# Cross-attention of a Perceiver layer: probabilities turned ahead of the scores in every step, and copied ahead of the maximum

## The chip, the cores and the metric

The kernel runs on one core of one Trainium2 chip. Its engines work side by side, each through its own instructions in order: TensorE (PE, and PEld for its weight loads), VectorE (DVE), ScalarE (ACT), GpSimd (POOL) and SyncE (SP), which issues the loads and stores. They wait for each other by semaphores. The metric is the device time of one execution in microseconds (us), and the number that is compared is the median of several executions.

## What is computed

The layer has three parts: cross-attention of 4096 rows over a context, causal self-attention, and a mixture of 8 experts. The change touches the first part alone.

```python
def _L0_xattn_ref(x, context, Wq, Wk, Wv, Wo, bo):
    HEADS = 16; DIM_HEAD = 64; SCALE = DIM_HEAD ** (-0.5)
    q = x @ Wq            # x: 64 x 64 x 256
    k = context @ Wk      # context: 64 x 256 x 192
    v = context @ Wv
    ...                   # each split into 16 heads of 64
    sim = jnp.einsum('bhid,bhjd->bhij', q, k) * SCALE
    attn = jax.nn.softmax(sim, axis=-1)
    out = jnp.einsum('bhij,bhjd->bhid', attn, v)
    out = out.transpose(0, 2, 1, 3).reshape(B, Nq, INNER_DIM)
    return out @ Wo + bo

x = x + _L0_xattn_ref(_layernorm(x), ctx_768, ...)   # then self-attention, then the experts
```

## The kernel before

Rows are worked on in tiles of 128, that is two batches of 64 rows with 256 keys each, so there are 32 tiles, and two tiles (u = 0 and u = 1) make a group. `run_tiles` writes group 0 out (its first tile is special, `first=True`), runs a loop of 14 times over groups 1 to 14, writes group 15 out, and ends with a short drain. A tile is 8 steps p = 0 to 7, one for each pair of heads, and there are 16 steps in a group.

Products that need more than one pass are made of a rounded part (hi) and a rest (lo). Keys are never projected: the key weights are absorbed into the queries. For each pair and each half h there is one such unit of work, here called an absorption: TensorE multiplies `q_sb` by `wkt` into the bank `qk_ps` (or `o_ps`, for the three that are called early), ScalarE rounds it into `qk_hi` (`absorbed_hi`), and VectorE writes the rest into `qk_lo` and `qk_hi` (`absorbed_lo`, two instructions). Only then may TensorE put the next absorption into `qk_ps`: `absorb` waits for `qk_done`.

What TensorE does in a step of a tile that is not the first, in this order (`tile` under `@block.tensor`):

- the scores of the pair before, ten matmuls into one of two banks `s_ps` (`scores`)
- in some steps the projection of a query pair, six matmuls into `m_ps` (`project_q`; steps 0, 2, 4 of u = 0 and 0, 1, 2, 4, 6 of u = 1)
- the values, five matmuls into `v_ps`
- in steps 1 and 2 of u = 1 an early absorption into `o_ps`
- the transposes of the probabilities of the pair three back, four into `t_ps` (line 555). They wait for `norm_done` from GpSimd two steps back and for `t_done`, VectorE's copy of the transposes before
- in steps 3 and 7 the product of probabilities and values, 64 matmuls into `o_ps` (line 571)
- in step 4 the output projection, 24 matmuls into `y_ps`
- in nearly all steps of u = 0 but the last, and of u = 1 but the first, a late absorption into `qk_ps`, the last work of the step

VectorE in a step: the negated maximum of the scores (`nmax`, line 733), the rest of the absorption that TensorE made at the end of the step before (`unit_behind`), the rest of the projected query (`q_lo`), the rest of an early absorption, in one step of a group `xt_lo`, the copy of the transposes from `t_ps` to `pt_sb` (line 754), the reciprocal of the sums (line 757, after ScalarE's exponentials), and what belongs to single steps: `ot_lo` in steps 3 and 7, the output rows in 5, `rem_lo` in 6, the layer norm of the next group in steps 0 (statistics) and 2 of u = 0.

ScalarE in a step: the rounded part of the absorption behind, of the projected query (`q_hi`), the two exponentials (line 667), the copy of the values, the rounded part of an early absorption. GpSimd scales the probabilities by the reciprocal (line 412). The order is written by hand; in all engines it is program order.

Of the kernel before, what the change touches and what calls it, by code (L numbers as in the profile page):

```python
# [22 lines left out]
P = 128  # L23
# [7 lines left out]
def wait(eng, sem, value):  # L31

    if isinstance(value, int) and value <= 0:
        return
    eng.wait_ge(sem, value)
# [38 lines left out]
def layer_kernel(nc, x, ctx_t, wq, wk, wv, wo, bo, sq, sk, sv, so, router, w_gate, w_up, w_down, out):  # L74
# [7 lines left out]
    PAIRS = E // P  # L82
# [8 lines left out]
    with ExitStack() as root:  # L91
# [9 lines left out]
        ident = sbuf(root, "ident", [P, P])  # L101
# [113 lines left out]
        with ExitStack() as ph:  # L215
# [229 lines left out]
            def _(pe):  # L445
# [66 lines left out]
                def tile(t, u, first, last, look, drain=False):  # L512
                    for p in range(PAIRS):
# [7 lines left out]
                        if first and p == 1:  # L521
                            pe.wait_ge(s_ctx, 3)
                            pe.wait_ge(s_rem, 1)
                        if (not first if p < LAG_S else cur):
                            scores(t, u, p, n, w)
# [22 lines left out]
                        if p == PAIRS - 1 and u == 0 and look:  # L548
                            turn_x(t // 2 + 1)
                        if (not first if p < LAG_T else cur):  # L550

                            pe.wait_ge(norm_done, n - 2)
                            wait(pe, t_done, n - 3)
                            for k in range(4):
                                mm = pe.transpose(t_ps[:, k * P:(k + 1) * P],  # L555
                                                  p_sb[:, (p - 3) % 4, k * P:(k + 1) * P], ident[:])
                            mm.then_inc(t_mm, 1)
                        if p % 4 == 3 and (not first if p < LAG_PV else cur):
# [138 lines left out]
            def _(dve):  # L697
# [24 lines left out]
                def tile(t, u, first, last, look, drain=False):  # L722
                    for p in range(PAIRS):
# [5 lines left out]
                        if first:  # L729
                            absorbed_lo(*early[:3], two_banks=True)  # L730
                        if (not first if p < LAG_S else cur):
                            dve.wait_ge(s_mm, n)
# [14 lines left out]
                        if p == PAIRS - 1 and u == 0 and look:  # L747
                            xt_lo_copy(t // 2 + 1)
                        if (not first if p < LAG_T else cur):
                            dve.wait_ge(t_mm, n - 2)  # L750
                            wait(dve, pv_mm, PAIRS * t - (0 if p >= LAG_PV else 4))
                            if first and p == LAG_T:
                                weights.wait_split(dve, O_SPLIT)
                            nc.vector.tensor_copy(pt_sb[:, PT_SLOT[(p - 3) % PAIRS], :], t_ps[:]).then_inc(t_done, 1)  # L754
                        if (not first if p < LAG_S else cur):
# [1016 lines left out]
```

## Time and profile before

| | us |
|---|---|
| median of 3 runs | 2334.02 |
| lowest and highest | 2332.64, 2343.82 |
| the profiled execution | 2338.02 |
| its span, first to last instruction | 2336.3 |
| PE busy in the span | 2202.6 |
| DVE busy | 1595.0 |
| ACT busy | 1283.4 |

The profiled execution is 4.0 us above the median. Cross-attention goes from the start to about 1236 us, self-attention to about 1880, the experts to the end. Within cross-attention one group of 16 steps follows the other: from the scores of step 4 at 501.06 us to the same place at 575.55 us it is 74.5 us. Matmuls are pipelined, so their durations overlap; the pace of TensorE is read from start to start.

### The profile page before, as it was taken

The numbers are of one execution on the slowest core, as the hardware profiler recorded it, in microseconds if no ns is written. First come the engines' busy times: TensorE is split into PE (matmuls) and PEld (weight loads), VectorE is DVE, ScalarE is ACT, GpSimd is POOL, SyncE is SP. The second block draws the span as 40 slices with busy tenths as digits, with TensorE's granted clock in tenths as the row PEclk, the third lists the DMA queues.
The fourth block names the chain that finished last, engine by engine and source line by source line (L and its number), as shares of the span: only waits on it lengthen the run. The fifth ranks groups of instructions, "written<-read, shape, count | busy, mean of one in ns | idle before, by whom it ended". The sixth has DMA issues, their size and how long they took to land. (4 is left out here: it accounts for less than half of the span.)

```text
span 2336.3 us, 55684 instructions
## 1 busy us (share of the span) xinstructions
PE 2202.6 (94%) x18992; PEld 1991.8 (85%) x18992; DVE 1595.0 (68%) x3591; ACT 1283.4 (55%) x3842; POOL 847.2 (36%) x1022
## 2 busy tenths in 40 slices
PE   6999999999999999999996999999999956999995
PEld 5899999999999999999985999999999844888884
DVE  6666676766667676666655888888898756444442
ACT  5555555555555555555544666676766622444442
POOL 3333333333333333333331222222222223777673
PEclk9999999999999999999997999999999976999998
DMA  4000000000000000000004000000000011434434
GB/s 115 19 20 27 9 27 27 18 27 9 27 18 27 13 22 27 18 27 9 14 6 154 11 10 18 9 18 9 18 9 19 19 39 48 105 79 104 78 54 104
DMA packets 61946, 82.52 MB, mean 35 GB/s; under 512 B 9936, under 2 KB 45520, under 8 KB 61808
## 3 DMA queue, kind: packets, MB, share of 16 engines
q1 hardware_dynamic: 48912, 63.46, 8.6%
q0 software_dynamic: 12960, 18.12, 4.7%
q8 instruction: 40, 0.66, 0.1%
q14 instruction: 34, 0.28, 0.0%
HBM read 59.80 MB, written 25.96 MB: 37 GB/s over the span
## 5 line engine op out<-in xcount | busy, mean ns | idle before, releaser
L412 POOL TENSOR_TENSOR p_sb<-p_sb,rinv 128x512 f32<-128x512 f32 x256 | 279.5, 1092 | 781.3 <-DVE rinv L757 781.3
L667 ACT ACTIVATE p_sb<-s_ps,nmax 128x256 f32<-128x256 f32 x512 | 238.3, 470 | 198.7 <-DVE nmax L733 194.8
L733 DVE TENSOR_REDUCE nmax<-s_ps 128x2 f32<-128x512 f32 x256 | 176.3, 689 | 186.6 <-PE s_ps L65 182.2
L914 POOL TENSOR_TENSOR sp_sb<-sp_sb,srinv 128x512 f32<-128x512 f32 x128 | 133.4, 1042 | 426.1 <-DVE srinv L1108 426.1
L1056 ACT ACTIVATE sp_sb<-sm_sb,snmax 128x128 f32<-128x128 f32 x512 | 199.4, 390 | 7.1 <-DVE snmax L1119 4.0
L754 DVE COPY pt_sb<-t_ps 128x512 f32<-128x512 f32 x256 | 177.0, 691 | 22.1 <-PE t_ps L555 8.5
L46 ACT ACTIVATE q_sb<-m_ps 64x256 fp32r<-64x256 f32 x256 | 97.0, 379 | 164.1 <-PE m_ps L65 160.3
L45 ACT CAST qk_hi<-qk_ps 128x512 fp32r<-128x512 f32 x218 | 129.8, 595 | 96.1 <-PE qk_ps L65 88.3
L555 PE MATMUL t_ps<-ident,p_sb 128*128 128x128 f32 x1024 | 153.8, 273 | 2.1 <-POOL p_sb L412 1.1
L555 PEld LDWEIGHTS t_ps<-ident,p_sb 128*128 128x128 f32 x1024 | 125.0, 141 | 31.8 <-issue 4.5
L638 ACT COPY v_sb<-v_ps 128x512 f32<-128x512 f32 x256 | 149.4, 584 | 1.5 <-PE v_ps L65 1.5
L65 PE MATMUL s_ps<-cx_hi,qk_hi 128*128 128x256 f32 x512 | 148.4, 290 | 0.0
L65 PE MATMUL qk_ps<-q_sb,wkt_hi 128*128 128x256 f32 x436 | 131.8, 324 | 14.3 <-DVE qk_hi L57 6.0
L65 PE MATMUL s_ps<-cx_lo,qk_hi 128*128 128x256 f32 x512 | 145.0, 283 | 0.0
L65 PE MATMUL s_ps<-cr_lo,qk_hi 128*128 128x256 f32 x512 | 144.9, 283 | 0.0
L65 PE MATMUL s_ps<-cx_hi,qk_lo 128*128 128x256 f32 x512 | 144.8, 283 | 0.0
L65 PE MATMUL s_ps<-cr_hi,qk_hi 128*128 128x256 f32 x512 | 144.8, 283 | 0.0
L571 PEld LDWEIGHTS o_ps<-pt_sb,v_sb 128*64 128x64 f32 x4096 | 126.2, 139 | 11.6 <-issue 10.5
L571 PE MATMUL o_ps<-pt_sb,v_sb 128*64 128x64 f32 x4096 | 135.1, 225 | 0.8 <-DVE pt_sb L754 0.8
L58 DVE SCALAR_TENSOR_TENSOR q_sb<-m_ps,q_sb 64x256 fp32r<-64x256 f32 x256 | 108.1, 422 | 37.6 <-ACT q_sb L46 30.9
L1570 POOL DMA_INDIRECT acc<-e_ys,e_token_out x67 | 107.3, 1601 | 23.1 <-issue 18.6
L65 PE MATMUL qk_ps<-q_sb,wkt_lo 128*128 128x256 f32 x436 | 113.9, 283 | 0.0
(300 smaller groups left out, 7581.7 us busy)
## 6 DMA issues: line engine op xcount, KB each, us to landing
ctx_raw<-in_ctx_t SPq DMA_DIRECT2D x32, 256.0 KB, 2.8
ctx_raw<-in_ctx_t SPq DMA_DIRECT2D x64, 128.0 KB, 3.0
x_ring<-in_x SPq DMA_DIRECT2D x16, 256.0 KB, 2.8
x_mid<-x_ring SPq DMA_DIRECT2D x16, 256.0 KB, 2.2
xn<-f_xn SPq DMA_DIRECT2D x16, 256.0 KB, 2.2
acc<-x_sb SPq DMA_DIRECT2D x16, 256.0 KB, 2.3
e_raw<-in_gate SPq DMA_DIRECT2D x8, 512.0 KB
e_raw<-in_up SPq DMA_DIRECT2D x8, 512.0 KB
```

Of the source, the lines that this page charges most:

```text
L45: return nc.scalar.copy(hi, src)
L58: return nc.vector.scalar_tensor_tensor(out=lo, in0=src, scalar=scale, in1=f32(hi), op0=ALU.mult, op1=ALU.subtract)
L65: mm = pe.matmul(out, lhs, rhs, start=(i == 0), stop=(i == len(pairs) - 1))
L412: nc.gpsimd.tensor_tensor(prob, prob, inv, ALU.mult).then_inc(norm_done, 1)
L555: mm = pe.transpose(t_ps[:, k * P:(k + 1) * P], p_sb[:, (p - 3) % 4, k * P:(k + 1) * P], ident[:])
L571: mm = pe.matmul(o_ps[h * HEAD:(h + 1) * HEAD, c:c + HEAD], v_sb[:, k, q * P + h * HEAD:q * P + (h + 1) * HEAD], pt_sb[:, PT_SLOT[q], k * ...
L638: nc.scalar.copy(v_sb[:, p % 4, p // 4 * HALF:(p // 4 + 1) * HALF], v_ps[:]).then_inc(v_done, 1)
L667: ex = nc.scalar.activation(p_sb[:, k, b * J:(b + 1) * J], s_ps[1 - w][:, b * J:(b + 1) * J], ACT.Exp, bias=nmax[:, k, b:b + 1], scale=1.0 ...
L733: nc.vector.tensor_reduce(nmax[:, (p - 1) % 4, :], s_ps[1 - w][:].rearrange("p (b j) -> p b j", b=2), AX_X, ALU.max, negate=True).then_inc ...
L754: nc.vector.tensor_copy(pt_sb[:, PT_SLOT[(p - 3) % PAIRS], :], t_ps[:]).then_inc(t_done, 1)
L914: nc.gpsimd.tensor_tensor(prob, prob, inv, ALU.mult).then_inc(norm_done, 1)
L1056: ex = nc.scalar.activation(p_sb[:, s, k * P:(k + 1) * P], sm_sb[:, w, k * P:(k + 1) * P], ACT.Exp, bias=nmax[:, s, k:k + 1], scale=1.0, a ...
```

## The change

On TensorE the block of four transposes moves from behind the values (and the early absorption) to the head of the step, ahead of `scores`. On VectorE the copy of these transposes moves from behind the rests to ahead of the maximum. No instruction is added or taken away, and all semaphores and the values that are waited for stay.

```diff
@@ TensorE, tile @@
+                        if (not first if p < LAG_T else cur):
+
+                            pe.wait_ge(norm_done, n - 2)
+                            wait(pe, t_done, n - 3)
+                            for k in range(4):
+                                mm = pe.transpose(t_ps[:, k * P:(k + 1) * P],
+                                                  p_sb[:, (p - 3) % 4, k * P:(k + 1) * P], ident[:])
+                            mm.then_inc(t_mm, 1)
                         if (not first if p < LAG_S else cur):
                             scores(t, u, p, n, w)
...
-                        if (not first if p < LAG_T else cur):
-
-                            pe.wait_ge(norm_done, n - 2)
...
@@ VectorE, tile @@
+                        if (not first if p < LAG_T else cur):
+                            dve.wait_ge(t_mm, n - 2)
+                            wait(dve, pv_mm, PAIRS * t - (0 if p >= LAG_PV else 4))
+                            if first and p == LAG_T:
+                                weights.wait_split(dve, O_SPLIT)
+                            nc.vector.tensor_copy(pt_sb[:, PT_SLOT[(p - 3) % PAIRS], :], t_ps[:]).then_inc(t_done, 1)
                         if (not first if p < LAG_S else cur):
                             dve.wait_ge(s_mm, n)
...
-                            nc.vector.tensor_copy(pt_sb[:, PT_SLOT[(p - 3) % PAIRS], :], t_ps[:]).then_inc(t_done, 1)
```

TensorE, end of step 5 and start of step 6 of a tile u = 1, before (`qk_ps` is the late absorption, `s_ps` the first of the next step's scores, the names in brackets are the semaphores waited for):

```order
L65 MATMUL v_ps<-wv_rem,cr_lo 128x512
L555 MATMUL t_ps<-ident,p_sb 128x128 [waits x_t_copied,x_norm]
L555 MATMUL t_ps<-ident,p_sb 128x128 x3
L65 MATMUL qk_ps<-q_sb,wkt_hi 128x256 [waits x_qk_split,x_q_split]
L65 MATMUL qk_ps<-q_sb,wkt_lo 128x256
L65 MATMUL qk_ps<-q_sb,wkt_hi 128x256
L65 MATMUL qk_ps<-q_sb,wkt_lo 128x256
L65 MATMUL s_ps<-cx_hi,qk_hi 128x256 [waits x_exp]
```

The same place after the change:

```order
L65 MATMUL v_ps<-wv_rem,cr_lo 128x512
L65 MATMUL qk_ps<-q_sb,wkt_hi 128x256 [waits x_qk_split,x_q_split]
L65 MATMUL qk_ps<-q_sb,wkt_lo 128x256
L65 MATMUL qk_ps<-q_sb,wkt_hi 128x256
L65 MATMUL qk_ps<-q_sb,wkt_lo 128x256
L529 MATMUL t_ps<-ident,p_sb 128x128 [waits x_t_copied,x_norm]
L529 MATMUL t_ps<-ident,p_sb 128x128 x3
L65 MATMUL s_ps<-cx_hi,qk_hi 128x256 [waits x_exp]
```

The transposes no longer stand between the values and the late absorption, but between the late absorption and the next scores.

VectorE, steps 5 and 6 of a tile u = 1 before, from the maximum of step 5 on:

```order
L733 TENSOR_REDUCE nmax<-s_ps 128x2 [waits x_s_mm]
L57 TENSOR_TENSOR qk_lo<-qk_ps,qk_hi 128x4x64 [waits x_qk_hi]
L57 TENSOR_TENSOR qk_hi<-qk_ps,qk_hi 64x4x64
L754 COPY pt_sb<-t_ps 128x512 [waits x_pv_mm,x_t_mm]
L757 RECIPROCAL rinv<-rsum 128x2 [waits x_exp]
L764 TENSOR_TENSOR x_ring<-y_ps,x_ring 128x256 [waits x_y_mm]
L733 TENSOR_REDUCE nmax<-s_ps 128x2 [waits x_s_mm]
```

The same place after, from the copy of step 5 on:

```order
L736 COPY pt_sb<-t_ps 128x512 [waits x_pv_mm,x_t_mm]
L739 TENSOR_REDUCE nmax<-s_ps 128x2 [waits x_s_mm]
L57 TENSOR_TENSOR qk_lo<-qk_ps,qk_hi 128x4x64 [waits x_qk_hi]
L57 TENSOR_TENSOR qk_hi<-qk_ps,qk_hi 64x4x64
L757 RECIPROCAL rinv<-rsum 128x2 [waits x_exp]
L764 TENSOR_TENSOR x_ring<-y_ps,x_ring 128x256 [waits x_y_mm]
```

The copy stands ahead of the maximum, and the reciprocal follows the rests directly.

## Rows read from the trace of the kernel before

**Rows 1.** The page's first part: busy time, share of the span, instructions.
```profile
PE 2202.6 (94%) x18992; PEld 1991.8 (85%) x18992; DVE 1595.0 (68%) x3591; ACT 1283.4 (55%) x3842; POOL 847.2 (36%) x1022
```

**Rows 2.** Stretches: length, PE, PEld, DVE, ACT, POOL busy, PEclk, DMA share, GB/s.
```profile
20.00:60.00 40.00, 31.68 (x198) 28.66 (x199) 32.36 (x68) 24.56 (x59) 9.33 (x11) 1.00 0.22 64
...
427.50:1171.50 744.00, 740.12 (x7239) 680.24 (x7238) 507.52 (x1122) 415.57 (x1170) 260.53 (x250) 1.00 0.07 20
```

**Rows 3.** Waits from 60 to 1225 us: total us, times, longest.
```profile
DVE nmax L733 <- PE s_ps L65: 181.7, 143, 3.6
...
PEld qk_ps L65 <- DVE qk_hi L57: 17.5, 56, 0.7
PEld o_ps L571 <- issue: 10.5, 63, 0.2
...
PE qk_ps L65 <- DVE qk_hi L57: 6.0, 14, 0.4
```

**Rows 4.** TensorE in time, steps 5 and 6 of u = 1: start, length, instruction.
```profile
544.66 0.28 PE L65 MATMUL qk_ps<-q_sb,wkt_hi 128*128 128x256 f32 x1
...
545.14 0.28 PE L65 MATMUL s_ps<-cx_hi,qk_hi 128*128 128x256 f32 x1
...
546.34 0.40 PE L65 MATMUL v_ps<-wv_hi,cx_hi 128*128 128x512 f32 x1
...
547.51 0.60 PE L555 MATMUL t_ps<-ident,p_sb 128*128 128x128 f32 x4
548.06 0.39 PE L65 MATMUL qk_ps<-q_sb,wkt_hi 128*128 128x256 f32 x1
...
548.64 0.28 PE L65 MATMUL s_ps<-cx_hi,qk_hi 128*128 128x256 f32 x1
...
552.08 0.36 PE L65 MATMUL qk_ps<-q_sb,wkt_hi 128*128 128x256 f32 x1
```

**Rows 5.** VectorE in time, step 5 of the same tile; in brackets the idle time before.
```profile
546.54 0.69 DVE L733 TENSOR_REDUCE nmax<-s_ps 128x2 f32<-128x512 f32 x1 [3.55 <-PE s_ps L65]
547.15 0.42 DVE L57 TENSOR_TENSOR qk_lo<-qk_ps,qk_hi 128x256 fp32r<-128x256 f32 x1
547.58 0.43 DVE L57 TENSOR_TENSOR qk_hi<-qk_ps,qk_hi 64x256 fp32r<-64x256 f32 x1
548.14 0.69 DVE L754 COPY pt_sb<-t_ps 128x512 f32<-128x512 f32 x1
```

**Rows 6.** TensorE, then VectorE, in group 15, where scores follow transposes directly.
```profile
1192.35 0.60 PE L555 MATMUL t_ps<-ident,p_sb 128*128 128x128 f32 x4
1192.70 0.36 PE L65 MATMUL s_ps<-cx_hi,qk_hi 128*128 128x256 f32 x1
...
1194.18 0.69 DVE L733 TENSOR_REDUCE nmax<-s_ps 128x2 f32<-128x512 f32 x1 [0.43 <-PE s_ps L65]
```

**Rows 7.** Steps 0 and 1 of u = 0, with the layer norm: ScalarE, VectorE, TensorE.
```profile
561.95 0.20 ACT L667 ACTIVATION_READ_ACCUMULATOR p_sb<-s_ps,nmax 128x1 f32 x1
...
562.75 0.17 DVE L757 RECIPROCAL rinv<-rsum 128x2 f32<-128x2 f32 x1
...
563.98 0.69 DVE L733 TENSOR_REDUCE nmax<-s_ps 128x2 f32<-128x512 f32 x1
...
565.50 0.39 PE L65 MATMUL qk_ps<-q_sb,wkt_hi 128*128 128x256 f32 x1 [0.43 <-DVE qk_hi L57]
```

**Rows 8.** VectorE in step 2 of u = 1, then TensorE's late absorption.
```profile
530.60 0.67 DVE L733 TENSOR_REDUCE nmax<-s_ps 128x2 f32<-128x512 f32 x1
...
531.62 0.43 DVE L57 TENSOR_TENSOR qk_hi<-qk_ps,qk_hi 64x256 fp32r<-64x256 f32 x1
...
532.24 0.36 PE L65 MATMUL qk_ps<-q_sb,wkt_hi 128*128 128x256 f32 x1
```

**Rows 9.** GpSimd in time: the scaling of the probabilities whose scores began at 545.14.
```profile
549.11 1.04 POOL L412 TENSOR_TENSOR p_sb<-p_sb,rinv 128x512 f32<-128x512 f32 x1 [5.00 <-DVE rinv L757]
```

**Rows 10.** A stretch in the drain; columns as in rows 2.
```profile
1225.60:1229.40 3.80, 3.68 (x64) 3.50 (x64) 0.01 (x1) 0.00 (x1) 0.00 (x0) 0.50 0.02 4
```

More of the change, by code:

```diff
@@ L549, in tile @@
                             turn_x(t // 2 + 1)
-                        if (not first if p < LAG_T else cur):
-                            pe.wait_ge(norm_done, n - 2)
[L553 to L557, printed above, removed]
                         if p % 4 == 3 and (not first if p < LAG_PV else cur):
@@ L748, in tile @@
                             xt_lo_copy(t // 2 + 1)
[L749 to L753, printed above, removed]
-                            nc.vector.tensor_copy(pt_sb[:, PT_SLOT[(p - 3) % PAIRS], :], t_ps[:]).then_inc(t_done, 1)
                         if (not first if p < LAG_S else cur):
```

## The prediction

> **What bounds the kernel now.** The page comes first: TensorE is busy 94% of the span [rows 1]. The stretches then say where: over ten groups of cross-attention, 744 us, it is busy 740 at full clock, so the stage is paced by TensorE, and only what makes it wait or work longer can move the time [rows 2]. The list of waits names the one thing that it waits for in the steady loop: an absorption's first weight load waits for VectorE's second rest (`qk_hi`), 56 times, 17.5 us in all, that is 4 times in each of 14 groups [rows 3]. In the other direction VectorE waits for the scores before its maximum, 143 times, 181.7 us [rows 3].
>
> The timelines of TensorE and VectorE side by side explain this wait. In step 5 of u = 1 the scores start at 545.14, the maximum at 546.54, the two rests at 547.15 and 547.58, the second ends at 548.01, and the late absorption starts at 548.06 [rows 4, 5]. From the scores' start to the absorption that is a chain of 2.92 us, all of it forced: the maximum waited for the scores (idle 3.55 before), the rests stand behind the maximum, the absorption needs its bank freed. In the meantime TensorE issues scores (1.20), values (1.17) and transposes (547.51 on, 0.35 as from 1192.35 to 1192.70 in [rows 6]), 2.72 in sum. It is 0.20 short, and waits. So the transposes are what TensorE does while VectorE works through the chain; this is what the change takes away.
>
> **The tight steps.** After the change such a step is transposes, scores, values, then the absorption. The scores start 0.35 later, and the chain starts with them. It also grows a little: where scores follow transposes, the maximum starts 1.48 after them and not 1.40 [rows 4 to 6], since the first matmul runs longer (0.36 against 0.28). The step, from its first work to the next step's first, was 3.50 (545.14 to 548.64 [rows 4]); it becomes 0.35 + 2.92 + 0.08 + 0.58 (absorption to next step, 548.06 to 548.64) = 3.93, so +0.43. TensorE then stands idle some 0.6 in it. VectorE's copy doesn't lengthen the chain there: it can start 0.63 after the transposes (547.51 to 548.14 [rows 4, 5]) and lasts 0.69, so it is over at 1.32, and the maximum is due at 0.35 + 1.48 = 1.83; what hides the copy is VectorE's wait for the scores. Such steps have no projection, no product of 64 and no output projection between scores and absorption: steps 5 and 6 of u = 0 and step 5 of u = 1, three in each of 15 groups. 45 x 0.43 = **19.4 us**. Bounds: 0.35 (the longer first matmul is gained back elsewhere) and 0.55, 15.8 to 24.8.
>
> The Trainium skill bears on the 0.08: "TensorE: Matmul & The Clock Gate", Part 2, says that the engine's window pulls a weight load ahead of the matmuls in flight, so that it is hidden. By that rule the 0.08 would be zero and this term 15.8; the rows show it behind transposes.
>
> **The layer-norm step.** In steps 0 and 1 of u = 0 VectorE is late already: between reciprocal (562.75) and maximum (563.98) lie the layer norm's statistics, 1.23, with no idle time, and the absorption waits 0.43 [rows 7]. Now the copy comes between statistics and maximum: +0.72 (a copy and its distance to the next instruction). But the reciprocal no longer stands behind the copy; it needs the exponentials, ready at 562.15 [rows 7] and now 0.35 later, as the projection ahead of them moves back, so it can start near 562.55, 0.2 earlier. The maximum then starts at 562.55 + 1.23 + 0.72 = 564.50, with 0.06 for one more instruction of the sequencer between them 0.58 later than before, and so does the absorption, which waits for it. 14 x 0.58, and group 15 without statistics 0.43: **8.5 us**. Bounds 0.36 and 1.1 each, 5 to 15.
>
> **Steps 1 and 2 of u = 1.** VectorE has its longest backlog here: two queries' and two absorptions' rests. The maximum at 530.60 follows other work directly, and the second rest ends at 532.05, while the absorption that needs it started at 532.24, just unstalled [rows 8]; there is no fifth wait in a group [rows 3]. The chain behind this is projection, ScalarE's part, rests, copy, maximum; its head, the projection, now comes 0.35 after the step's start, where it had come first thing behind the scores. The rest ends near 0.4 later, which makes the absorption 0.2 to 0.35 late; I take 0.3. 15 x 0.3 = **4.5 us**. Bounds 0 (the second copy is out of the way) and a whole copy, 0.7: 0 to 10.
>
> **Steps that only trade places.** With a projection in it the step is not tight: in step 6 TensorE comes to the absorption 3.44 after the scores (548.64 to 552.08 [rows 4]), 3.09 without the transposes, 3.17 with the longer first matmul, and the chain needs 3.00. The cover is thin, 0.17 us: if it goes, three such steps a group (0 and 2 of u = 0, 6 of u = 1) cost what the chain lacks. An absorption behind values instead of transposes reaches the next step in 0.48 (544.66 to 545.14 [rows 4]) and not 0.56, which pays for the 0.08. The output projection of step 4 covers everything: 0. In the steps with the product of 64, TensorE now goes to it from the values. The trace has a gap of 0.17 ahead of each product, 10.5 us in 63 [rows 3], always behind transposes, whose matmuls are short. Whether it stays behind the longer values no row shows: -0.10 if it goes, +0.08 if it stays, times 62, so -6 to +5. I take **-1**.
>
> **First tile and drain.** Two stretches without the loop's rhythm. In the first tile VectorE is busy 32.4 of 40 us [rows 2] and paces it; the copy filled its pause between two absorptions and now lies in its chain, five steps from p = 3 on, some 0.5 each: **2.5 us** (0 to 3.5). In the drain the last scores' maximum waits behind one more copy, and the last transposes wait for the end of its chain, with nothing beside it: a copy's 0.69 [rows 5], **0.7 us**.
>
> **The waits that are only moved.** The transposes' own condition, `norm_done`, must now hold earlier. The scaling of the probabilities of scores 545.14 runs from 549.11 to 550.15 [rows 9]; its transposes are those of step 7, which starts at about 552.6. Over 2 us are left, so nobody waits. Behind them queue the scores, so this would be dear if it failed. No DMA moves: SP waits for `s_ctx`, `s_rem` and `bo_added`, which come from GpSimd work with idle time before it (5.00 us [rows 9]).
>
> **Sum.** 19.4 + 8.5 + 4.5 - 1 + 2.5 + 0.7 = 34.6. The profiled execution took 2338.0, so 2372.6; the median of the runs is 2334.0, 4.0 lower, and that is what will be compared: 2368.6. I say 2368.
>
> **The rivals.**
> - *The wait is VectorE's backlog, not the chain.* If the absorption waited because VectorE was still behind from copies of the step before, a copy moved into its idle time before the maximum would end the wait, and the kernel would gain up to all 17.5 of PEld's wait, 2317. It decides whether the maximum starts late or on time. On time in the tight steps (idle 3.55 before it [rows 5]), late only in the layer-norm step; against it. Chance 0.03.
> - *Nothing to measure.* The stalls come, but are paid back: the gap of 0.17 vanishes (-6), a step that stalls lets VectorE catch up, and the late steps cost nothing. 15.8 + 5 + 0 - 6 - 5 = about 10, 2344. Chance 0.07. That the change doesn't do what it says is out: the order shows the absorption right behind the values.
> - *The thin cover breaks.* If the 45 steps with a projection and no other cover also wait, and lose as much as the tight ones do, 0.4 each, that is 18 us more, 2386. For it: the cover is 0.17, and VectorE has further work in them. Against it: that work stands behind the rests, not ahead. Chance 0.09.
> - *The clock falls.* TensorE now pauses 0.6 us several times a group. In the trace the granted clock stays 1.00 from 20 to 60 us though TensorE is idle a fifth of it [rows 2]; at 0.50, in the drain, the product of 64 takes 3.68 us [rows 10]. A twentieth of the stage at that level would cost some 58 us, 2426. Chance 0.02. The Trainium skill, in the same page under "A second HAM failure mode: psum-queue depth-cycling", says that frequent short pauses between groups of matmuls make the clock swing between its levels; by this trace they don't.
>
> **How the numbers follow.** The forecast, 2350 to 2383, has the remaining 0.79. The low bounds, 15.8 + 5 + 0 - 6 + 0 + 0.7, give 15.5, so 2350; the high ones together would be 59, but not all at once, and I stop at 50, 2384. Range 2350 to 2384. The measurement tells about 0.5% (11.7 us) from no change: slower than that 0.90, within 0.07, faster 0.03.
>
> **What would show it.** In the profile after, a group takes 76.3 to 77 us and not 74.5; PEld's wait for `qk_hi` rises from 17.5 to some 50, in five steps a group and not four, about 0.6 in the tight ones; the maximum still starts 1.48 after the scores in steps 5 and 6; the granted clock of the loop is 1.00; PEld waits for no `p_sb`. If the group is not longer, the chain was not forced; if `o_ps` has no gap any more, that term goes down by 5.

## The result, and the profile after

The changed kernel takes 2377.48 us, the median of 4 runs (2373.95 to 2379.01); the kernel before, run beside it, 2334.56 (2332.64 to 2343.82). The ratio is 1.017, with a 95% interval of 1.015 to 1.0188: slower by 42.9 us. 2368 was forecast, 34.6 above the kernel before. The profiled execution took 2377.52, and its span is 2375.8.

First the page of the changed kernel, its part on busy time, to set against [rows 1]; then the stretches, as in [rows 2] (length, PE, PEld, DVE, ACT, POOL busy, PEclk, DMA share, GB/s), of which the long one is ten groups again:

```profile
PE 2205.7 (93%) x18992; PEld 1985.9 (84%) x18992; DVE 1591.9 (67%) x3591; ACT 1281.2 (54%) x3842; POOL 847.0 (36%) x1022
```

```profile
20.00:60.00 40.00, 31.54 (x211) 28.33 (x211) 32.89 (x70) 23.78 (x57) 9.88 (x11) 1.00 0.20 64
427.50:1197.00 769.50, 743.93 (x7250) 678.97 (x7249) 508.79 (x1125) 416.12 (x1171) 262.95 (x251) 1.00 0.06 19
```

The same numbers of instructions do the same work in the same busy time. What is new is idle time of TensorE: 25.6 us in ten groups, where it was 3.9 in [rows 2]. A group takes 76.95 us instead of 74.5, and the granted clock of TensorE is 1.00 in both stretches as the rows print it; for 20 to 60 us the matmuls say otherwise (see the rivals, below).

The list of waits of the changed kernel from 60 to 1225 us (total, times, longest) names the place, beside [rows 3]:

```profile
DVE pt_sb L736 <- PE t_ps L529: 110.0, 76, 2.9
...
DVE nmax L739 <- PE s_ps L65: 63.1, 137, 0.5
PEld qk_ps L65 <- DVE qk_hi L57: 59.2, 56, 1.8
...
PE qk_ps L65 <- DVE qk_hi L57: 38.9, 74, 1.3
...
PEld o_ps L571 <- issue: 19.3, 61, 0.4
...
DVE ln_stats_x L164 <- issue: 3.0, 14, 0.2
```

The absorption's wait for VectorE's second rest is the one that grew: from 17.5 to 59.2 us on PEld, and from 14 to 74 times on PE, which is some five a group. VectorE's long wait is now at its copy, the first thing in a step that needs TensorE, and no longer at the maximum. No wait for the scaled probabilities is in the list up to 1225 us.

A tight step of the changed kernel, step 5 of u = 1, on TensorE (start, length, instruction, in brackets the idle time), against [rows 4]:

```profile
558.71 0.60 PE L529 MATMUL t_ps<-ident,p_sb 128*128 128x128 f32 x4
559.06 0.36 PE L65 MATMUL s_ps<-cx_hi,qk_hi 128*128 128x256 f32 x1
...
560.33 0.40 PE L65 MATMUL v_ps<-wv_hi,cx_hi 128*128 128x512 f32 x1
...
562.05 0.38 PE L65 MATMUL qk_ps<-q_sb,wkt_hi 128*128 128x256 f32 x1 [0.39 <-DVE qk_hi L57]
...
562.63 0.60 PE L529 MATMUL t_ps<-ident,p_sb 128*128 128x128 f32 x4
```

and VectorE in the same step, against [rows 5]:

```profile
559.34 0.69 DVE L736 COPY pt_sb<-t_ps 128x512 f32<-128x512 f32 x1 [2.92 <-PE t_ps L529]
560.53 0.69 DVE L739 TENSOR_REDUCE nmax<-s_ps 128x2 f32<-128x512 f32 x1 [0.50 <-PE s_ps L65]
561.14 0.41 DVE L57 TENSOR_TENSOR qk_lo<-qk_ps,qk_hi 128x256 fp32r<-128x256 f32 x1
561.57 0.43 DVE L57 TENSOR_TENSOR qk_hi<-qk_ps,qk_hi 64x256 fp32r<-64x256 f32 x1
```

From transposes to transposes it is 3.92 us, with the scores at 0.35, the maximum 1.47 behind them, and the absorption 2.99 behind them. The copy is over at 560.03, and VectorE still waits 0.50 for the scores: the copy costs nothing here. The values' last matmul starts near 561.27 (560.33 and four of 0.23), so TensorE has some 0.55 with nothing new to start.

The layer-norm step of the changed kernel, on VectorE, against [rows 7], and then on TensorE:

```profile
576.59 0.17 DVE L757 RECIPROCAL rinv<-rsum 128x2 f32<-128x2 f32 x1 [0.19 <-ACT p_sb L667]
576.97 0.75 DVE L164 BATCH_NORM_STATS2 ln_stats_x<-x_ring 128x6 f32 x2 [0.21 <-issue]
...
578.24 0.69 DVE L736 COPY pt_sb<-t_ps 128x512 f32<-128x512 f32 x1
578.85 0.68 DVE L739 TENSOR_REDUCE nmax<-s_ps 128x2 f32<-128x512 f32 x1
```

```profile
576.44 0.36 PE L65 MATMUL s_ps<-cx_hi,qk_hi 128*128 128x256 f32 x1
...
580.35 0.39 PE L65 MATMUL qk_ps<-q_sb,wkt_hi 128*128 128x256 f32 x1 [1.31 <-DVE qk_hi L57]
...
581.28 0.36 PE L65 MATMUL s_ps<-cx_hi,qk_hi 128*128 128x256 f32 x1
```

TensorE waits 1.31 for the rest, where [rows 7] had 0.43. From scores to scores this step takes 4.84 us; before, the same places are 562.11 and 566.07, 3.96.

### The profile page after: what moved, and what is told of

The parts are those of the page before. It is cut to its first block and busy times, and to the rows that moved or that the text cites. A ratio compares the mean times of both kernels' runs of the same rounds, so it can differ in the third digit from the quotient of the medians.

```text
span 2375.8 us, 55684 instructions
## 1 busy us (share of the span) xinstructions
PE 2205.7 (93%) x18992; PEld 1985.9 (84%) x18992; DVE 1591.9 (67%) x3591; ACT 1281.2 (54%) x3842; POOL 847.0 (36%) x1022
## 5 line engine op out<-in xcount | busy, mean ns | idle before, releaser
L65 PE MATMUL qk_ps<-q_sb,wkt_hi 128*128 128x256 f32 x436 | 126.0, 311 | 48.4 <-DVE qk_hi L57 38.9
L65 PE MATMUL s_ps<-cx_hi,qk_hi 128*128 128x256 f32 x512 | 164.7, 322 | 0.0
L65 PEld LDWEIGHTS qk_ps<-q_sb,wkt_hi 128*128 128x128 f32 x436 | 82.3, 189 | 88.2 <-DVE qk_hi L57 59.2
L58 DVE SCALAR_TENSOR_TENSOR q_sb<-m_ps,q_sb 64x256 fp32r<-64x256 f32 x256 | 108.1, 422 | 36.8 <-ACT q_sb L46 30.2
L529 PEld LDWEIGHTS t_ps<-ident,p_sb 128*128 128x128 f32 x1024 | 118.3, 140 | 6.8 <-POOL p_sb L412 2.5
```

What stands on the lines that cost most here:

```text
L58: return nc.vector.scalar_tensor_tensor(out=lo, in0=src, scalar=scale, in1=f32(hi), op0=ALU.mult, op1=ALU.subtract)
L65: mm = pe.matmul(out, lhs, rhs, start=(i == 0), stop=(i == len(pairs) - 1))
L529: mm = pe.transpose(t_ps[:, k * P:(k + 1) * P], p_sb[:, (p - 3) % 4, k * P:(k + 1) * P], ident[:])
```

## The experiments

The theory is the chain of the prediction: scores, maximum, two rests, absorption. It sets the length of some steps, and more so since the transposes no longer stand inside it. A length of a step is given below from the start of its values to the start of the next step's values, unless it says otherwise; on that measure a tight step is 3.49 before and 3.92 after (4.22 and 4.65 where it holds the next step's projection).

The first five kernels move both parts in some steps of a tile only. Their edit is one condition, and both blocks stand in both places, under it and under its opposite:

```diff
+            def ahead(t, u, p, first, drain):
+                return not first and not drain and (u, p) in ((0, 5), (0, 6), (1, 5))
...
+                        if ahead(t, u, p, first, drain) and (not first if p < LAG_T else cur):
+                            pe.wait_ge(norm_done, n - 2)
...
-                        if (not first if p < LAG_T else cur):
+                        if not ahead(t, u, p, first, drain) and (not first if p < LAG_T else cur):
```

**The three tight steps alone.** The edit is the one shown.

> The new order (transposes ahead of the scores, copy ahead of the maximum) in three steps of a group only: 5 and 6 of u = 0 and 5 of u = 1, that is 45 steps; all else as before. My theory (the transposes were what TensorE did while VectorE worked through maximum and rests, 2.92 us, and moved ahead they lengthen the step by themselves and the slower first matmul): each such step 3.93 instead of 3.50, a group 75.8 instead of 74.5, the kernel +19.4 us, near 2354. Rival (the copy on VectorE, and not the transposes' place, costs the time, and costs it in the steps where VectorE is late): these steps have VectorE idle before the maximum, so they stay at 3.50 and the kernel at 2334.6.

Measured: 2359.54 us (2357.66 to 2361.2, 4 runs) beside 2337.87; ratio 1.0089 (1.0061 to 1.0117). A group takes 75.73 us, +1.24, which is 3 x 0.41. From the first scores to the last transposes the stage is 19.1 us longer. The waits of this kernel from 60 to 1225 us:

```profile
DVE nmax L751 <- PE s_ps L65: 96.1, 141, 1.1
...
PEld qk_ps L65 <- DVE qk_hi L57: 44.2, 56, 0.8
```

PEld's wait goes up by 26.7 us, with the maximum waiting for the scores about as often as before (141 times for 143). The forecast of 19.4 for this part holds.

**Steps 0 and 1 of u = 0 alone** (`u == 0 and p < 2`), the layer-norm step.

> The new order in steps 0 and 1 of u = 0 only, where the layer norm's statistics stand between reciprocal and maximum. My theory: the changed kernel's trace shows 4.84 from the scores of step 1 to those of step 2 instead of 3.97, of which the copy between statistics and maximum is 0.6 to 0.7 and the rest the wait of the statistics' own instructions (0.38 from reciprocal to statistics, 0.08 before), which the copy had hidden; so 14 x 0.87 and 0.43 in group 15: +12.6 us, near 2347. Rival (the steps lose only what the transposes' place takes, 0.43 as in any tight step): 15 x 0.43 = +6.4 us, near 2341.

Measured: 2351.56 us (2347.18 to 2354.1, 5 runs), ratio 1.006 (1.0038 to 1.0082). The group is 75.34, +0.85, and the stage 12.5 longer. `DVE ln_stats_x <- issue: 3.0, 14, 0.2` is in its list, as in the changed kernel's and not in the list of before.

**Steps 1 and 2 of u = 1 alone** (`u == 1 and p in (1, 2)`).

> The new order in steps 1 and 2 of u = 1 only, where VectorE has two absorptions' and two queries' rests. My theory: the absorption at the end of step 2 waits about 0.5 us for a rest that now ends later; 15 x 0.31 = +4.7 us, near 2339, and the group 74.8 instead of 74.5. Rival (the changed kernel's longer step 2 is a consequence of the steps before it): with the steps before and after in the old order nothing is left, 2334.6.

Measured: 2366.51 us (4 runs), ratio 1.0124 (1.0096 to 1.0151); group 76.08, +1.6 and not +0.31. The expectation was missed, and its waits show why:

```profile
PEld t_ps L533 <- issue: 20.1, 16, 1.3
...
PE t_ps L533 <- DVE pt_sb L772: 16.8, 16, 1.1
```

Where step 0 is in the old order and step 1 in the new one, the transposes of the two stand almost side by side, and there is one bank `t_ps`. The second four wait for the copy of the first, 1.1 us, once a group. This wait belongs to the seam and is in neither whole kernel, so the run says nothing about the term.

**All steps but these** (the opposite of the three conditions together, first tile and drain included).

> The new order in all steps but those three sets (5, 6, 0, 1 of u = 0 and 5, 1, 2 of u = 1 in the steady groups), so also in the first tile and the drain. My theory: these steps have cover (a projection, the product of 64, the output projection), 0 in the group, under 1 us in the first tile and 0.4 in the drain: +0.5 to +2 us, 2335 to 2337. Rival (some 6 us of the 42.9 have their place outside the three sets, in the tile's rhythm or in later stages that depend on it): +6 us or more, 2341.

Measured: 2404.87 us (4 runs), ratio 1.0284 (1.0255 to 1.0312). It has the same flaw, several times a group: `PE t_ps L533 <- DVE pt_sb L772: 37.4, 43, 2.2`, and groups of 77.7 and 79.3 in turn. As a measure of "the rest costs nothing" it is inconclusive. The turns are of another kind, and they bear on the rival of the clock. Once a group TensorE waits 2.17 for the copy, and behind this wait the granted clock falls in every second group:

```profile
242.60 0.91 PE L533 MATMUL t_ps<-ident,p_sb 128*128 128x128 f32 x4 [2.17 <-DVE pt_sb L772]
```

```profile
242.80:246.20 3.40, 3.40 (x16) 3.30 (x15) 1.21 (x2) 0.00 (x0) 1.97 (x2) 0.50 0.00 0
```

The second row is a stretch, with columns as in [rows 2]. At 0.50 the matmuls of the scores start 0.21 apart and not 0.12, and the group with such a stretch is the one of 79.3.

**Steps 0 to 3 of u = 1** (`u == 1 and p < 4`): a seam where the step before ends with a late absorption and a product of 64 covers the other end.

> The new order in steps 0 to 3 of u = 1 only. The run with steps 1 and 2 alone had two blocks of transposes closer together than before: those of step 0 in the old place at the end, those of step 1 at the head, so that TensorE waited for the copy in between (16.8 us in 16 waits). Here the new order begins behind a step that ends with the product of 64 and an absorption. My theory: the group 74.8 (+0.31), all of it in step 2, and no wait of the transposes for the copy; 15 x 0.31, near 2342 beside 2338. Rival (the wait for the copy belongs to the new order itself): the group 76 again, +24 us.

Measured, one run: 2346.38 beside 2337.97; group 74.90, +0.41, stage +7.2. No transposes wait for a copy more than 0.2. The step from step 2 to 3 is 4.13, as in the changed kernel, where before had 3.74. So the 0.39 of this step is real; what its seams add (6.69 for 6.16 at one end, 5.76 for 6.21 at the other) leaves this part between 0.31, read in the whole change, and 0.41.

**The transposes moved, the copy left where it was** (only the first half of the change's diff).

> TensorE's transposes ahead of the scores in every step as in the change, VectorE's copy left in the old place behind the rests. My theory says that the transposes' place alone opens the tight steps (+0.43 each) whatever VectorE does, and that the copy's place was needed to go with it: the next transposes at the head of a step would wait for a copy that stands behind the rests, about 0.15 us in the three tight steps and 0.9 in the six with a projection, so that the group is 80 us or more, and the kernel 2410 to 2450. Rival (the copy ahead of the maximum is what made the changed kernel slower): the group is shorter than the changed kernel's 76.95, near 75, and the kernel near 2345.

Measured, one run: 2560.63 us, groups of 88 and 89.5. The list of waits of this kernel:

```profile
PEld t_ps L529 <- issue: 153.3, 131, 2.8
PE t_ps L529 <- DVE pt_sb L754: 129.7, 90, 2.6
```

The direction was expected, the size was not: I had 2410 to 2450. With transposes at the head and the copy behind the rests, the next step's head waits for the end of this step's chain, up to 2.6 us, and 11 of the 16 steps of a group are longer than before. The granted clock falls to 0.50 in this kernel too, at the end of some of the waits of 2.5 us (from 448.5 to 451.9 us, for one). So the copy's new place is what saves the change from something far worse. The other half, the copy moved without the transposes, was not tried on the chip.

**The chain cut, in the kernel before.** If the chain through the maximum is the limit, the rests should go ahead of the maximum, since they need only the absorption behind:

```diff
+                        if behind is not None:
+                            absorbed_lo(*behind[:3], two_banks=False)
                         if (not first if p < LAG_S else cur):
                             dve.wait_ge(s_mm, n)
                             nc.vector.tensor_reduce(nmax[:, (p - 1) % 4, :], ...)
-                        if behind is not None:
-                            absorbed_lo(*behind[:3], two_banks=False)
```

> The kernel before, with one edit: VectorE writes the rest of the absorption behind ahead of the maximum and not behind it; transposes and copy stay in the old place. My theory (TensorE waits at the late absorption because the rests stand behind a maximum that must wait for the scores): the wait of 17.5 us goes, the three tight steps take 3.28 instead of 3.50, the layer-norm step loses its 0.4, a group 73.3 instead of 74.5, and the kernel is 17 us faster than before, 2321 beside 2338. The maximum starts 0.3 later, which nothing waits for. Rival (the rests are late because of ScalarE's rounding or VectorE's load, whatever their order; or the later maximum is passed on through the exponentials and the values' copy): the group stays at 74.5 or grows.

Measured: 2338.00 us (2333.85 to 2341.4, 10 runs) beside 2337.97; ratio 0.9992 (0.998 to 1.0004), no change. The wait for `qk_hi` is gone from the list, the tight steps take 3.27 and not 3.49, the layer-norm step 4.11 and not 4.67, and then one step, 3 of u = 1, gives 0.9 of the 1.2 back (7.11 for 6.20): `PE t_ps L555 <- DVE pt_sb L754: 11.6, 16, 1.0`. Steps 2 and 3 of u = 0 give back another 0.2, which leaves a group of 74.37 for 74.49. The mechanism was right, the sum was not.

**The same in the changed kernel**, where the copy comes first, then the rests, then the maximum.

> The changed kernel, with the same one edit: copy, rest of the absorption, maximum. My theory: with the rests no longer chained to the scores, the place of the transposes makes no difference in the tight steps, which take 3.28 as in the other run; only the layer-norm step, where copy and rest stand behind the statistics, still waits 0.5 to 1.0. A group 73.8 to 74.3 instead of 76.95, the kernel 2325 to 2335 beside 2338 and 2377. Rival (the loss of the change is VectorE's work, 0.7 us of copy ahead of everything else in a step): the group stays near 76.9, since the copy is still first.

Measured: 2333.42 us (2330.35 to 2338.97, 10 runs), ratio to the kernel before 0.9981 (0.9968 to 0.9995). This is the run that decides. Transposes are ahead of the scores and the copy ahead of the maximum as in the change, and the loss of 1.7% is gone: group 74.14 instead of 76.95. Step 5 of u = 1, on TensorE and then on VectorE:

```profile
546.68 0.60 PE L529 MATMUL t_ps<-ident,p_sb 128*128 128x128 f32 x4
...
549.47 0.28 PE L65 MATMUL qk_ps<-q_sb,wkt_hi 128*128 128x256 f32 x1
...
549.94 0.60 PE L529 MATMUL t_ps<-ident,p_sb 128*128 128x128 f32 x4
```

```profile
547.32 0.69 DVE L736 COPY pt_sb<-t_ps 128x512 f32<-128x512 f32 x1 [1.57 <-PE t_ps L529]
...
548.35 0.43 DVE L57 TENSOR_TENSOR qk_hi<-qk_ps,qk_hi 64x256 fp32r<-64x256 f32 x1
```

The second rest is over 0.7 before the absorption needs it, and the step takes 3.26. With the rests ahead in both orders, the tight steps take 3.27 in the old order and 3.26 to 3.31 in the new one, and step 2 of u = 1 takes 3.74 in both. So in these steps neither the place of the transposes nor that of the copy costs anything by itself; what costs is that the rests stand behind a maximum that comes late.

The layer-norm step is different. It remains at 5.00, and 28 waits for `qk_hi` with it, where the old order with the rests ahead has 4.11:

```profile
565.55 0.69 DVE L736 COPY pt_sb<-t_ps 128x512 f32<-128x512 f32 x1
566.16 0.41 DVE L57 TENSOR_TENSOR qk_lo<-qk_ps,qk_hi 128x256 fp32r<-128x256 f32 x1
566.59 0.43 DVE L57 TENSOR_TENSOR qk_hi<-qk_ps,qk_hi 64x256 fp32r<-64x256 f32 x1
```

Here VectorE goes from the statistics to the copy and from the copy to the rests without a pause, so the copy's new place (0.61 to the next instruction) is part of the 0.9. That the groups of the two kernels are nearly equal all the same (74.37 and 74.14) is because the old order pays 0.9 in step 3 of u = 1 instead.

**Why the layer-norm step lost 0.87 and not 0.58.** Two kernels on the changed one. The first moves the next group's statistics from step 0 of u = 0 to step 4, with their `rstd` in 5 and the application in 6 (the other two conditions change alike):

```diff
-                        if p == (3 if first else 0) and u == 0 and look:
+                        if p == (3 if first else 4) and u == 0 and look:
```

> The changed kernel with the layer norm's statistics moved from step 0 to step 4 of u = 0 (reciprocal deviation and application to 5 and 6). My theory of why the layer-norm step lost 0.87 and not 0.43: the reciprocal, with the copy gone from ahead of the statistics, exposes the sequencer's own instructions, and the late statistics stand in the chain. Without them this step should lose only what a tight one loses: group 76.4 to 76.6 us instead of 76.95, kernel some 5 to 7 us under the changed one. Rival: the 0.87 comes from the copy's new place or the transposes, not from the statistics; then the group stays at 76.9 or more.

Measured: 2360.31 us (2358.73 to 2368.09, 4 runs), ratio to the kernel before 1.0092 (1.0066 to 1.0118). The group is 76.03, not 76.95, and it fell by more than I expected: the whole step goes from 5.55 to 4.64. That is what such a step takes elsewhere in this kernel (4.65). Before the change the same comparison is 4.67 against 4.22. So 0.43 of the 0.87 is what any step of this kind loses, and 0.45 is the statistics, whose price went from 0.45 to 0.91 (4.67 - 4.22, 5.55 - 4.64).

The second puts the copy back behind the rests in step 1 of u = 0 only:

```diff
-                        if (not first if p < LAG_T else cur):
+                        if (first or u or p != 1) and (not first if p < LAG_T else cur):
...
+                        if not (first or u or p != 1) and (not first if p < LAG_T else cur):
+                            dve.wait_ge(t_mm, n - 2)
```

> The changed kernel with VectorE's copy put back behind the rests in one step of a group, step 1 of u = 0; the transposes stay at the head. My theory: there the copy lies on the chain (statistics, copy, maximum, rests, absorption) and costs about 0.6 to 0.7; put behind, the maximum comes that much earlier, and the transposes of step 2 have to wait for the copy a little, 0.1 to 0.3. Group 76.4 to 76.6 us instead of 76.95. Rival: VectorE's wait for the scores covers the copy in that step as in the tight ones; then nothing is gained and the group is 77.0 or more.

Measured, one run: 2377.07 us; the group is 76.63, -0.32, and the step 5.24. Over 14 groups, from the values of step 4 of u = 1 in group 0 to the same place in group 14, the kernel is 4.3 us shorter than the changed one (1072.9 for 1077.2). That the total does not show it lies in part in the first tile, which took 2.6 us longer in this execution (63.4 from the first scores to the first product of 64, against 60.9); the granted clock was 0.50 there from 45.2 to 48.6 us, and it was not in the changed kernel. VectorE in this kernel:

```profile
578.99 0.17 DVE L763 RECIPROCAL rinv<-rsum 128x2 f32<-128x2 f32 x1 [0.19 <-ACT p_sb L667]
579.37 0.76 DVE L164 BATCH_NORM_STATS2 ln_stats_x<-x_ring 128x6 f32 x2 [0.21 <-issue]
...
580.64 0.69 DVE L739 TENSOR_REDUCE nmax<-s_ps 128x2 f32<-128x512 f32 x1
...
582.14 0.69 DVE L760 COPY pt_sb<-t_ps 128x512 f32<-128x512 f32 x1
```

The maximum follows the statistics at once, 0.61 earlier than with the copy between. Half of that shows in the group; the next transposes start 0.24 later behind the absorption than elsewhere, since they wait for the late copy. So the copy's new place costs 0.3 here, net. The 0.38 from reciprocal to statistics stays with the copy gone from there: it isn't the copy's.

**A version that beats both.** In the kernel before, the rests ahead of the maximum only where TensorE waits for them, and not in the step that gave the gain back:

```diff
+            def rest_first(u, p):
+                return (u, p) in ((0, 1), (0, 5), (0, 6), (1, 5))
...
+                        if behind is not None and rest_first(u, p):
+                            absorbed_lo(*behind[:3], two_banks=False)
...
-                        if behind is not None:
+                        if behind is not None and not rest_first(u, p):
```

> The kernel before with the second rest of the absorption behind put ahead of the maximum in four steps only (1, 5, 6 of u = 0 and 5 of u = 1) and everything else as it was. My theory: the chain from the scores to the next absorption is scores, maximum, rests; taking the rests out of it saves 0.22 us in each of three steps and about 0.56 between the layer-norm step and the next, and the step that lost 0.9 when the edit was made everywhere (3 of u = 1) is not touched. Group 73.3 to 73.5 us instead of 74.5, kernel 15 to 17 us under the kernel before. Rival: what was gained there is only handed on, the next wait (for the exponentials or for the transposes' bank) takes it back in the following step; then group 74.3 or more and the kernel within 4 us of before.

Measured: 2321.2 us (2313.8 to 2325.71, 6 runs) beside 2339.71; ratio 0.9907 (0.9887 to 0.9927), 18.5 us faster. The group is 73.24. The stretch, columns as in [rows 2], and VectorE in the layer-norm step:

```profile
427.50:1171.50 744.00, 744.00 (x7373) 690.52 (x7372) 520.40 (x1139) 417.57 (x1189) 264.90 (x253) 1.00 0.06 21
```

```profile
553.71 0.69 DVE L760 COPY pt_sb<-t_ps 128x512 f32<-128x512 f32 x1
554.43 0.17 DVE L763 RECIPROCAL rinv<-rsum 128x2 f32<-128x2 f32 x1
554.51 0.73 DVE L164 BATCH_NORM_STATS2 ln_stats_x<-x_ring 128x6 f32 x2
...
555.69 0.42 DVE L57 TENSOR_TENSOR qk_lo<-qk_ps,qk_hi 128x256 fp32r<-128x256 f32 x1
556.13 0.43 DVE L57 TENSOR_TENSOR qk_hi<-qk_ps,qk_hi 64x256 fp32r<-64x256 f32 x1
556.59 0.69 DVE L739 TENSOR_REDUCE nmax<-s_ps 128x2 f32<-128x512 f32 x1
```

TensorE is busy in all of the 744 us, and no wait of it for `qk_hi` is left in the list. From reciprocal to statistics it is 0.08 again, since here the reciprocal did not wait.

**The same with the statistics in step 4.**

> As rest_first_in_four, and the layer norm's statistics moved from step 0 to step 4 of u = 0, with its reciprocal deviation a step and its application two steps behind them (5 and 6). My theory: steps 0 and 1 then have no statistics between reciprocal and maximum, so what is left of their excess over the rhythm of the others goes; step 4 has the output projection as cover and takes the statistics free. Group 73.1 to 73.3 us, kernel 16 to 20 us under the kernel before. Rival: step 4 is itself full on VectorE, the statistics only change the place of the stall; group 73.5 or longer, no better than rest_first_in_four.

Measured: 2330.26 us (2328.46 to 2332.45, 6 runs), ratio 0.9954 (0.9935 to 0.9972): better than before, worse than without the second edit. Steps 0 and 1 gain the hoped-for 0.12 (3.99 for 4.11), but at the end of the tile a step takes 7.17 for 6.16: `PE m_ps L475 <- DVE ln_xn_x L184: 11.1, 14, 0.8`. It is not step 4 that is full, as the rival had it; the normalised rows, applied in step 6, come too late for TensorE's transposes of them. The application should have stayed early, which the statistics in step 4 don't allow.

## Why the prediction was right, and where its sum was off

The time lies in the range, and the mechanism was the one forecast for the steady loop; that the sum came near is in part because its errors have different signs. Point by point, from the two traces, with the stage taken from the first scores (10.50 before, 9.05 after) to the last transposes:

```profile
1224.15 0.74 PE L555 MATMUL t_ps<-ident,p_sb 128*128 128x128 f32 x4 [1.05 <-POOL p_sb L412]
```

```profile
1259.41 0.79 PE L529 MATMUL t_ps<-ident,p_sb 128*128 128x128 f32 x4 [2.25 <-POOL p_sb L412]
```

The first row is of the kernel before, the second of the changed one. The ends are 1224.89 and 1260.20, so the stage is 36.8 us longer.

- **Tight steps**, 19.4 forecast. In the trace 3.50 became 3.92, over all 45 steps it is 19.2, and the experiment alone gave 19.1. Each number of the step came as worked out: scores at 0.35, maximum 1.47 later (1.48 forecast), 0.58 from absorption to next step, some 0.55 of pause for the 0.6.
- **Layer-norm step**, 8.5 forecast, measured 0.87 in the group shown and 12.4 over 14 groups, with 0.4 in group 15; 12.5 in all in the run of its own. This is the term that was most mis-sized. The step that failed is the one that let the statistics start 0.08 behind the reciprocal, as they did when the reciprocal ran straight behind the copy. Counted from the step's first work, the maximum was forecast at 2.45 and started at 2.76: the reciprocal 0.06 later than forecast, the statistics 0.30 later behind it (0.38, of which the list of idle time calls 0.21 "issue"), statistics to copy 0.06 longer (1.27 against the 1.15 from the statistics of before, below, to the maximum of [rows 7], and the 0.06 that I gave), copy to maximum 0.11 shorter (0.61). In all, 0.31. Over the kernels above it is 0.37 to 0.40 in each group of the five in which the reciprocal had waited for the exponentials, and 0.08 in each group of those in which it followed a copy; so much is shown. That it is the sequencer's own work ahead of the statistics (their waits on values counted in the loop), done behind the copy's back in the one case and after the wait in the other, is argued; no run took one of these waits away. The Trainium skill, "Perfetto Trace Analysis", section "DVE / Act Engine Instruction (TENSOR_ADD, Activation, etc)", has the sequencer pushing instructions into a queue of waiting ones and going on to the next; by that rule such work is hidden as long as the engine is busy with what is queued, and this trace agrees for the case with the copy. The row of the kernel before:

```profile
562.83 0.73 DVE L164 BATCH_NORM_STATS2 ln_stats_x<-x_ring 128x6 f32 x2
```

- **Steps 1 and 2 of u = 1**, 4.5 forecast. Read between the two traces it is 0.31 a group, 4.6. The experiment meant to take it alone failed at its seam, and the better one gave 0.41 with its own seams in it. So the size rests on the traces of the whole change. That it belongs to the same chain, the run with the rests ahead in the changed kernel shows: step 2 is back at 3.74 there.
- **Places traded**, -1 forecast. Steps with a projection take 3.27 before and after, and the thin cover held. The gap ahead of the product of 64 neither vanished nor stayed: from the last matmul of the values (510.54) to the product (510.87) it is 0.33, where the pace of the values is 0.23, so 0.10 is left of the 0.17 behind transposes. PEld's list has more in this row than before (19.3 for 10.5), though the step didn't get longer: that row counts idle time of the weight loads, which can lie beside the values still running. The three lines of the balance (gap, longer first matmul, shorter way behind values) are not separated; what the terms above leave of the 36.3 between the first product of 64 and the last output projection is -0.3.
- **First tile and drain**, 2.5 and 0.7 forecast, measured 1.4 and 0.4. From the start of the first values to the first product of 64 it is 36.13 before (35.12 to 71.25) and 37.51 after (32.41 to 69.92). It is 36.1 in six kernels above (the kernel before is one of them) with the old order in the first tile, and 37.5 in four with the new one; in the other four the granted clock was 0.50 for a stretch near 45 us, and they have 1.4 to 1.6 more. Why it is 1.4 and not 2.5 no run shows. From the first scores to the product the two traces differ by 0.1 only (60.75 and 60.87), because the first values come 1.3 sooner in the changed kernel's execution (23.4 behind the first scores, for 24.6). Nothing that was changed stands ahead of them, and kernels with the old order have 23.3 as well as 24.8. In the drain the last transposes wait 2.25 for GpSimd and not 1.05, as the rows above show. From the last tile's output projection, behind which there is no absorption and so no tight step, to their end it is 18.80 and 19.17.

Together 19.2 + 12.8 (layer norm, with group 15) + 4.6 - 0.3 + 1.4 + 0.4 = 38.1 for the change, beside the 34.6 of the forecast: 4.3 too little for the layer-norm step, 0.7 that wasn't gained by places traded, 1.4 too much for first tile and drain. With the 1.3 of the sooner first values taken off it is 36.8, which is what the stage shows.

The two profiled executions are 39.5 us apart: the 36.8 of the stage, 1.5 less ahead of it, 1.0 less between it and the experts, and 5.2 more in these. From the first expert matmul (1960.13 before, 1994.46 after) to the end it is 376.1 and 381.3 us, with the same code; over the kernels above, which all have the same code there, it is 375.1 to 385.5 in no order of what was changed. The other 3.4 of the 42.9 are there because the kernel before was profiled in an execution 3.5 above its median. The kernel before by itself gave medians from 2334 to 2340 in the runs beside these. A forecast of this change can't be tested closer than that by totals; the length of a group can, to a few hundredths.

The rivals: that the wait was VectorE's backlog falls with the tight steps alone, where the wait grew though the copy went into idle time. The thin cover didn't break. The clock didn't fall in the loop of the changed kernel: the granted clock stayed at 1.00 through pauses of 0.4 and 1.3 us several times a group. The Trainium skill's rule on pauses between groups of matmuls ("TensorE: Matmul & The Clock Gate", "A second HAM failure mode: psum-queue depth-cycling") would have had it swing. The trace of the changed kernel disagrees, but two of the variants agree: with a wait of 2.17 once a group the granted clock fell in every second group (all steps but these), and it fell at the end of waits of 2.5 in the kernel with the transposes alone moved. So the rival was wrong for this change, by its own trace, and not for every kernel of this kind.

One reading in the prediction's argument against this rival was wrong. It took the granted clock to be 1.00 from 20 to 60 us [rows 2]. The matmuls of the kernel before start 0.21 apart up to 33 us, as they do at 0.50 above, and 0.12 apart from there:

```profile
32.75 0.41 PE L65 MATMUL s_ps<-cx_hi,qk_lo 128*128 128x256 f32 x1
32.96 0.41 PE L65 MATMUL s_ps<-cx_lo,qk_hi 128*128 128x256 f32 x1
...
33.49 0.28 PE L65 MATMUL y_ps<-q_sb,wkt_hi 128*128 128x256 f32 x1
33.61 0.28 PE L65 MATMUL y_ps<-q_sb,wkt_lo 128*128 128x256 f32 x1
```

So TensorE was at the lower level (1.2 GHz) for the first third of this stretch, and the row did not show it. In the changed kernel's execution the pace changes between 26.8 and 29.0 us, sooner behind its first scores than before; that this is where the first values gained their 1.3 is likely, and no run tested it.

## What to carry to other kernels

Before moving independent work out of a stretch, ask which chain it covered: here the four transposes, 0.35 us together, were the last thing that TensorE had to do while VectorE went from scores to rests, and ahead of the scores they cover nothing. The cheaper way out was on the other engine: put first what the bottleneck waits for (the rests), and last what only a slack engine waits for (the maximum), in the few steps where there is a wait, not in all. And when an instruction's predecessor changes from a busy one to a waiting one, add the longer distance between them, here 0.3 us; that it is the sequencer's work is not shown.

## What the runs showed of the hardware

- Distances on VectorE depend on whether the instruction before was waited for: from the reciprocal to the statistics 0.08 us where the reciprocal followed a copy directly, 0.38 where it had waited 0.2 for ScalarE, with 0.21 "issue" in the row.
- A single bank shared by two blocks of transposes set side by side costs 1.1 us (16 times) where VectorE's copy comes at its usual place, and up to 2.6, 90 times in the stage, where the copy stands behind the whole chain.
- The first matmul of the scores lasts 0.36 behind transposes and 0.28 otherwise, in the changed kernel as in [rows 6]; the first behind a wait lasts 0.38 or 0.39.
- Pauses of TensorE up to 1.31 us, several times a group, left the granted clock at 1.00 in the loop of the changed kernel. Behind a wait of 2.17 us, once a group, it was 0.50 from 242.8 to 246.2 us and again in every second group of that kernel, which made the group 1.6 us longer (79.3 for 77.7).
- In the first tile the new order takes 37.5 us from the first values to the first product of 64 and the old one 36.1, in ten kernels without a fall of the clock there; a total of one execution hides it.
